# Counting edges between nodes in a four-layer graph network: 128 edges and four destinations per item, four items to a PSUM bank

## The reference

```
edge_index = stack([src, dst])
# layer 0: norms = segment_sum(exp(scores), rows)[rows]; res = segment_sum(w * v, rows)
# layer 1: e = exp(edge_weights - segment_max(edge_weights, tgt)[tgt])
#          gamma = e / segment_sum(e, tgt)[tgt]
# layer 2: h_e = segment_sum(h[src], dst)
# layer 3: prop(h) = segment_sum(wn[:, None] * h[row], col), with deg = segment_sum(1, row)
```

## Time and profile before

| | |
|---|---|
| runs (us) | 1515.14, 1507.11, 1510.53; median 1510.53 |
| profiled execution | 1497.43 us, of which the span is 1495.7 us |
| mean granted TensorE clock | 0.93 |
| busy share of the span | PE 75%, PEld 44%, DVE 74%, ACT 49%, POOL 32% |
| chain that ended last, by engine | PE 41%, DVE 29%, ACT 18%, issue 7% |

### The profile page before, as it was taken

One profiled execution on the slowest core, in us unless ns is written; L12 is line 12 of the kernel. 1 busy time (PEld: TensorE's weight loads), 2 busy tenths in 40 slices (PEclk: granted clock), 3 DMA queues, 4 the chain that ended last, 5 costly groups with the idle time before them and its releaser, 6 DMA issues.

```text
span 1495.7 us, 25017 instructions
## 1 busy us (share of the span) xinstructions
PE 1121.4 (75%) x8719; PEld 662.8 (44%) x8719; DVE 1107.2 (74%) x1935; ACT 736.6 (49%) x1363; POOL 476.0 (32%) x217
## 2 busy tenths in 40 slices
PE   0772465777777897787878778788469799999993
PEld 0441243555444452122222122222259697778783
DVE  8883799899897446898998998888695554432376
ACT  1562343666665126988998899898210000001121
POOL 5101000011000006698999999898100000000000
PEclk9997687999999798999999999999689899999997
DMA  0001000000000242111111111111111100010111
GB/s 7 15 1 46 5 1 18 2 8 9 2 2 15 75 105 62 32 46 39 41 46 39 43 50 46 55 42 54 39 47 46 44 28 8 1 27 8 48 36 33
DMA packets 60616, 47.50 MB, mean 32 GB/s; under 512 B 30607, under 2 KB 58895, under 8 KB 60367
## 3 DMA queue, kind: packets, MB, share of 16 engines
q1 hardware_dynamic: 59022, 44.04, 10.3%
q0 software_dynamic: 1472, 1.85, 0.5%
HBM read 32.07 MB, written 13.79 MB: 31 GB/s over the span
## 4 chain that ended last, share of the span: by engine, by line
PE 41%; DVE 29%; ACT 18%; issue 7%; SPq 2%; DMA 1%; POOL 1%; ACTq 1%; DVEq 0%
PE PS L1208 16%; DVE Eb L1015 11%; ACT CT L455 6%; ACT Eb L980 6%; ACT Eb L982 5%; PE PS L426 4%; PE PS L429 4%; DVE mov L358 3%; PE PS L1564 3%; PE PS L929 2%; PE PS L749 2%; PE PS L918 2%; DVE oneS L358 2%; ACT Eb L984 1%; POOL Eb L856 1%
## 5 line engine op out<-in xcount | busy, mean ns | idle before, releaser
L856 POOL TENSOR_SCALAR Eb<-Eb 128x1024 f32<-128x1024 f32 (+4 forms) x164 | 403.8, 2477 | 51.4 <-ACT Eb L984 51.0
L1015 DVE SCALAR_TENSOR_TENSOR Eb<-Eb,PS 128x1024 f32<-128x1024 f32 (+4 forms) x350 | 365.1, 1083 | 45.4 <-ACT Eb L982 35.2
L455 ACT ACTIVATE CT<-PS 128x200 f32 x783 | 236.6, 338 | 224.6 <-PE PS L429 222.6
L426 PE MATMUL PS<-mov,oneS 128*128 128x200 f16 x1566 | 245.2, 258 | 124.4 <-DVE mov L358 83.6
L1208 PE MATMUL PS<-hs,CT 128*128 128x192 f16 (+3 forms) x2500 | 269.8, 271 | 5.9 <-DVE B L1409 2.7
L984 ACT ACTIVATE Eb<-PS,small 128x1024 f32<-128x1024 f32 (+5 forms) x257 | 246.7, 995 | 22.7 <-PE PS L929 18.7
L1208 PEld LDWEIGHTS PS<-hs,CT 128*128 128x128 f16 (+1 forms) x2500 | 233.0, 101 | 39.4 <-DVE B L1409 3.2
L429 PE MATMUL PS<-CT,identb 128*128 x783 | 203.4, 260 | 29.1 <-ACT CT L455 28.2
L929 PE MATMUL PS<-Qb,Kb 96*128 96x512 f16 (+3 forms) x700 | 197.8, 365 | 13.1 <-ACT Eb L984 9.1
L426 PEld LDWEIGHTS PS<-mov,oneS 128*128 128x128 f16 x1566 | 138.4, 101 | 154.4 <-DVE mov L358 141.1
L358 DVE TENSOR_TENSOR mov<-iotaM,keyT 128x1600 f16<-128x1600 int16 x197 | 193.6, 983 | 0.0
(11 more groups left out here) (253 smaller groups left out, 937.5 us busy)
## 6 DMA issues: line engine op xcount, KB each, us to landing
Kb<-kd SPq DMA_DIRECT2D x168, 96.0 KB, 1.9
qd<-QH SPq DMA_DIRECT2D x24, 96.0 KB, 1.9
kd<-QH SPq DMA_DIRECT2D x24, 96.0 KB, 2.1
XG<-x_d SPq DMA_DIRECT2D x12, 192.0 KB, 2.4
x_d<-XG SPq DMA_DIRECT2D x12, 192.0 KB, 1.8
hs<-t_d SPq DMA_DIRECT2D x12, 192.0 KB, 2.5
Qb<-qd SPq DMA_DIRECT2D x4, 384.0 KB, 3.5
CT<-x_d SPq DMA_DIRECT2D x1, 1200.0 KB, 8.6
```

The lines of the kernel that those rows point to most:

```text
L426: t.matmul(ps, K.oneS[:, g % 2, 2 * k + s, :], K.mov[:, g % 2, 2 * k + s, :], start=(s == 0), stop=False)
L455: a.activation(K.CT[:, :, bass.ds(vals[p - 4 * g], W)], K.bank(p % 4)[:, 0:25 * W].rearrange("p (a w) -> p a w", w=W), ACT.Copy).then_inc( ...
L856: g.tensor_scalar(e, e, ELO, None, ALU.max).then_inc(S("floored"), 1)
L1015: v.scalar_tensor_tensor(out=e, in0=e, scalar=EHI, in1=cn, op0=ALU.min, op1=ALU.mult).then_inc(S("weighed"), 1)
```

## The change

Except for the length of a row of CT and the place of `ndis`, it stays within the count stage.

- A chunk has 128 edges and a window four destinations: 782 chunks, 784 windows, 1565 items, NJ = 13 slots, the second run from item LH = 792.
- Eight items (four of each run, now in blocks of four and not interleaved one by one) are a set; 198 sets. DVE makes one `oneS` (8 x 128) and one `mov` (8 x 100) per set, into three buffers (`DEEP`) instead of two.
- A half of a set is four items of one run, whose windows lie within 16 destinations. They share a bank: 25 x 16 columns. Each item has one count matmul, which writes its four columns of each 16 at an offset from a register (none for the first); then one CT matmul of 400 columns and one eviction of 400 columns. There are 392 halves. `load_windows` is called for each half: four registers on TensorE, one on ACT.
- The window numbers are relative within a half: `turnW` subtracts the first item's from the other three in the matmul that turns them. All are turned at the start, into `wI0` and `wI`.
- The chunk index of an item is found by seven comparisons of 1664 slots with chunk ends (`past`) and 7 + 42 matmuls that sum them over the partitions.
- The item arithmetic moves: DVE keeps the high and low parts (`high`), POOL computes the key, TensorE turns two tiles of 128 x 128, ACT copies them out of PSUM.
- The gathers have two buffers. CT is zeroed as POOL 7000, DVE 16000, ACT 16350 float32 elements per partition instead of 18500, 16000 and 4700. A row of CT has 12 columns more (NPC = 3148). `ndis` is a part of `small`.
- Softmax steps stand at sets 18, 26, ... 114, item turns at sets 6, 22, ...

```diff
-CH = 256
-NC = 392
+NPC = NP + 12
+CH = 128
+NC = 782
-W = 8
-WS = 3
-LH = 393
+W = 4
+WS = 2
+LH = 792
-NJ = 7
+NJ = 13
...
+SETS = 198
+DEEP = 3
+TURN_AT = {16 * (j - 1) + 6: j for j in range(1, NJ)}
+SOFT_AT = {18 + 8 * k: k for k in range(13)}
...
 def build_gpsimd(g, K):
...
+    g.memset(K.CTf[:, 0:ZG], 0.0).then_inc(S("zero_g"), 1)
...
+    g.wait_ge(S("slot_w"), 1)
+    gather(0)
     for j in range(NJ):
+        if j + 1 < NJ:
+            g.wait_ge(S("slot_w"), 2)
+            if j:
+                g.wait_ge(S("key"), j)
+                g.wait_ge(S("lo"), j)
+            gather(j + 1)
+        gd = K.GD[:, j % 2, :]
+        g.wait_ge(S("gd_in%d" % (j % 2)), 16 * (j // 2 + 1))
+        g.tensor_scalar(K.dl[:, :], gd, K.win[:, j:j + 1], 1.0, ALU.subtract, ALU.add).then_inc(own.sem, own.up())
+        g.wait_ge(own.sem, own.n)
+        g.tensor_scalar(K.over[:, :], K.dl[:, :], 1.0, None, ALU.is_ge).then_inc(own.sem, own.up())
+        g.tensor_scalar(K.under[:, :], K.dl[:, :], float(W), None, ALU.is_le).then_inc(own.sem, own.up())
+        g.wait_ge(S("hi"), j + 1)
+        g.tensor_scalar(K.key[:, :], K.hi[:, j % 2, :], 1.0, None, ALU.mult).then_inc(own.sem, own.up())
+        g.wait_ge(own.sem, own.n)
+        g.tensor_tensor(K.key[:, :], K.dl[:, :], K.key[:, :], ALU.add).then_inc(own.sem, own.up())
+        g.tensor_tensor(K.over[:, :], K.over[:, :], K.under[:, :], ALU.mult).then_inc(own.sem, own.up())
+        g.wait_ge(own.sem, own.n)
         if j:
...
+            g.wait_ge(S("key_turned"), j)
+        g.tensor_tensor(K.va[:, :], K.over[:, :], K.key[:, :], ALU.mult).then_inc(S("key"), 1)
...
 def build_vector(v, K):
...
+    for t in range(7):
+        v.tensor_scalar(K.past[:, t, :], K.iotaS[:, :], K.le[:, t:t + 1], None, ALU.is_gt).then_inc(S("past"), 1)
...
+    v.wait_ge(S("passed"), 1)
+    slots(slice(0, 1), K.bank(5)[:, 0:1])
+    v.wait_ge(S("passed"), 2)
+    slots(slice(1, NJ), K.bank(4)[:, 0:NJ - 1])
+    v.memset(K.CTf[:, ZG:ZV], 0.0).then_inc(S("zero_v"), 1)
+    v.wait_ge(S("windows"), 1)
+    v.tensor_copy(K.wI0[:, :], K.bank(5)[0:1, 128:256]).then_inc(S("reg_set"), 1)
...
+    for s in range(SETS):
+        j, o = s // 16, 8 * (s % 16)
+        v.wait_ge(S("items"), j + 1)
+        if s >= DEEP:
+            v.wait_ge(S("counted"), before(2 * (s - DEEP) + 2))
+        one_hots(K.oneS[:, s % DEEP, :, :], K.iotaX[:, :], K.KL[:, j, 1, o:o + 8, :], 128)
+        one_hots(K.mov[:, s % DEEP, :, :], K.iotaM[:, :], K.KL[:, j, 0, o:o + 8, :], 25 * W).then_inc(S("one_hot"), 1)
+        if s % 16 == 1 and j + 1 < NJ:
+            high(j + 1)
+        if s in SOFT_AT:
+            soft_step(SOFT_AT[s])
...
 def build_tensor(t, K):
...
+    for i, g in enumerate(PRESENT):
+        if i + 1 < len(PRESENT):
+            nxt = load_windows(K, t, mybir.EngineType.PE, PRESENT[i + 1], 4)
+        s, r = g // 2, g % 2
+        ps = bank(g % 4)[:, 0:25 * 4 * W].rearrange("p (a c) -> p a c", a=25)
+        t.wait_ge(S("one_hot"), s + 1)
+        if g >= 4:
+            t.wait_ge(S("placed"), INDEX[g - 4] + 1)
+        for k in range(items_of(g)):
+            to = ps[:, :, 0:W] if k == 0 else ps[:, :, bass.ds(vals[k], W)]
+            t.matmul(to, K.oneS[:, s % DEEP, 4 * r + k, :], K.mov[:, s % DEEP, 4 * r + k, :].rearrange("p (a w) -> p a w", a=25),
+                     start=(k == 0), stop=False, skip_group_check=True)
+        if g >= 2:
+            t.wait_ge(S("placed"), INDEX[g - 2] + 1)
+        t.matmul(ps, K.identb[:, :], K.CT[:, :, bass.ds(vals[0], 4 * W)], start=False, stop=True, skip_group_check=True
+                 ).then_inc(S("counted"), 1)
...
 def build_scalar(a, K):
...
+    def keep_items(j):
+        a.wait_ge(S("key_turned"), j + 1)
+        a.activation(K.KL[:, j, :, :, :].rearrange("p k i two -> p (k i) two"), bcast_in(K.bank(6)[:, 0:256], 256, 2), ACT.Copy
+                     ).then_inc(S("items"), 1)
...
+    for i, g in enumerate(PRESENT):
+        if i + 1 < len(PRESENT):
+            nxt = load_windows(K, a, mybir.EngineType.Activation, PRESENT[i + 1], 1)
+        s = g // 2
+        a.wait_ge(S("counted"), i + 1)
+        a.activation(K.CT[:, :, bass.ds(vals[0], 4 * W)],
+                     K.bank(g % 4)[:, 0:25 * 4 * W].rearrange("p (a c) -> p a c", a=25), ACT.Copy).then_inc(S("placed"), 1)
```

More of the change, by code:

```diff
@@ L91, in fl, with items_of, before @@
     return ap.rearrange("p t d -> p (t d)")
[L96 to L102, removed]
+SETS = 198
+SLOTS = NJ * 128
+PRESENT = [g for g in range(2 * SETS) if 4 * (g // 2) + LH * (g % 2) < NI]
+INDEX = {g: i for i, g in enumerate(PRESENT)}
+DEEP = 3
+TURN_AT = {16 * (j - 1) + 6: j for j in range(1, NJ)}
+SOFT_AT = {18 + 8 * k: k for k in range(13)}
+def items_of(g):
+    first = 4 * (g // 2) + LH * (g % 2)
+    return min(4, NI - first)
+def before(g):
+    return sum(1 for p in PRESENT if p < g)
 def alloc_build(K, st):
@@ L108, in alloc_build @@
     K.iotaX = sb(st, "iotaX", [128, 128], I16)
[L110 to L116, removed]
+    K.KL = sb(st, "KL", [128, NJ, 2, 128, 2], I16)
+    K.GS = sb(st, "GS", [128, 2, CH], I32)
+    K.GD = sb(st, "GD", [128, 2, CH], I32)
@@ L125, in alloc_build @@
[L125 to L135 removed]
+    K.lo = sb(st, "lo", [128, 2, CH], F32)
@@ L136, in alloc_build @@
+    K.le = sb(st, "le", [128, 7], F32)
+    K.cc = sb(st, "cc", [128, 7], I32)
+    with ExitStack() as st2:
+        K.iotaS = sb(st2, "iotaS", [128, SLOTS], I16)
+        K.past = sb(st2, "past", [128, 7, SLOTS], F16)
+    K.oneS = sb(st, "oneS", [128, DEEP, 8, 128], F16)
+    K.mov = sb(st, "mov", [128, DEEP, 8, 25 * W], F16)
     K.wv = sb(st, "wv", [128, J], F32)
@@ L203, in build_vector @@
     step = own.sem
[L204 to L208, removed]
+    v.memset(K.lw[:, 6:7], 32000).then_inc(S("lw_set"), 1)
+    v.memset(K.zf[:, :], 0.0).then_inc(S("zf"), 1)
+    v.memset(K.oneh[:, :], 1.0).then_inc(step, own.up())
+    v.wait_ge(S("iota"), 2)
@@ L211, in build_vector @@
     v.wait_ge(step, own.n)
[L212 to L215, removed]
+    v.scalar_tensor_tensor(out=K.pF[:, 1:2], in0=K.pI[:, 2:3], scalar=4.0 * LH, in1=K.pF[:, 0:1], op0=ALU.mult, op1=ALU.add
+                           ).then_inc(step, own.up())
@@ L230, in build_vector @@
[L230 to L262, removed]
-                              bcast_in(K.bank(6)[:, 256 + 128 * sub:384 + 128 * sub], 128, 2))
-            v.tensor_copy(K.wI[:, 128 * j:128 * j + 128], K.bank(4)[0:1, 0:128]).then_inc(S("items"), 1)
@@ new lines, in build_vector, with slots @@
+    first = K.identf[:, 0:128:4].unsqueeze(2).to_broadcast([128, 32, 3])
+    v.wait_ge(step, own.n)
+    v.tensor_tensor(K.turnW[:, :].rearrange("p (m k) -> p m k", k=4)[:, :, 1:4],
+                    K.identf[:, :].rearrange("p (m k) -> p m k", k=4)[:, :, 1:4], first, ALU.subtract).then_inc(step, own.up())
+    def slots(cols, ps):
+        v.scalar_tensor_tensor(out=K.win[:, cols], in0=ps, scalar=-4.0, in1=K.i4[:, cols], op0=ALU.mult, op1=ALU.add
+                               ).then_inc(step, own.up())
+        v.wait_ge(step, own.n)
+        v.tensor_scalar(K.cI[:, cols], ps, float(NC - 1), None, ALU.min).then_inc(S("slot_w"), 1)
@@ L383, in build_tensor @@
 def build_tensor(t, K):
     S, bank = K.S, K.bank
-    t.wait_ge(S("ends"), 1)
-    t.matmul(bank(0)[:, 0:NC - 1], K.onesf[0:1, :], K.lwF[:, NC:2 * NC - 1], start=True, stop=True).then_inc(S("ends_all"), 1)
+    for t_ in range(7):
+        t.wait_ge(S("past"), t_ + 1)
+        m = t.matmul(bank(5)[:, 0:1], K.past[:, t_, 0:128], K.oneh[:, :], start=(t_ == 0), stop=(t_ == 6))
+    m.then_inc(S("passed"), 1)
+    for j in range(1, NJ):
+        for t_ in range(7):
+            m = t.matmul(bank(4)[:, j - 1:j], K.past[:, t_, 128 * j:128 * j + 128], K.oneh[:, :], start=(t_ == 0), stop=(t_ == 6))
@@ L388, in turn_items @@
+    m.then_inc(S("passed"), 1)
+    t.wait_ge(S("slot_w"), 1)
+    t.matmul(bank(5)[0:1, 128:256], K.win[:, 0:1], K.turnW[:, :], start=True, stop=True).then_inc(S("windows"), 1)
+    t.wait_ge(S("slot_w"), 2)
+    t.matmul(bank(4)[0:NJ - 1, 128:256], K.win[:, 1:NJ], K.turnW[:, :], start=True, stop=True).then_inc(S("windows"), 1)
     def turn_items(j):
```

208 lines of the change are left out of this document (100 added, 108 removed).

## The result

| | before | after |
|---|---|---|
| runs (us), first chip | median 1510.53 (1506.50 to 1515.14, 7 runs) | median 1520.64 (1518.22 to 1525.06, 7 runs) |
| profiled execution (span) | 1497.43 (1495.7) | 1519.76 (1518.0) |
| mean granted clock | 0.93 | 0.81 |

The ratio is 1.0072, 95% interval 1.005 to 1.0093: slower, where 1485 was forecast and faster had 0.68. The result lies inside the range, on the wrong side of no change. So the change costs between 4 and 14 us, and 36 us lie between forecast and median on the first chip.

What follows compares the result with a forecast made beforehand. Bound: TensorE's own order of issue with ACT's loop in it. Count stage 372 + 37 + 7 = 416 against 439.6 (-23), preparation -2.5, total -25.6: 1472 for the profiled execution, 1485 for the median; range 1435 to 1528.

Steps and rivals of the forecast that it cites:

- TensorE per half: Count stage, TensorE's queue: register load gap of 0.51 plus four address steps of 0.11 make 0.95 us; bounds 0.75 and 0.99.
- h: Count stage: TensorE's time for a half of a set, four items; forecast 0.95 us.
- The gap: Count stage: from a CT matmul to the next first count matmul, register load included; 0.51 us, unchanged.
- The four steps: Count stage: three count matmuls and the CT matmul with register addresses, 0.11 us each, between 0.06 and 0.12.
- 352h + 82: Count stage time in us as a function of a half's time; 0.95 gives 416.
- Rival A: Count stage: TensorE's queue runs ahead and hides the address steps; half 0.75 us, -91.5 us, 1419 us; chance 0.20.
- Rival B: Count stage: TensorE's clock stays at its lower level; half 1.09 us, +24 us, 1534 us; chance 0.20.
- Rival C: Count stage: address steps at upper bound, or clock partly lower; half 1.00 to 1.045, about 1510 us; chance 0.12.
- Stalls: Count stage: softmax steps interrupting DVE, with three buffers as cover, cost TensorE 24.4, 2.6, 2.6 and 7.7, sum 37 us.
- ACT and DVE: Count stage: eviction of 400 columns 0.50 us, DVE set 1.08 us, ACT loop 1.07 per two halves; neither sets the pace.
- Preparation: Before the count stage: less zeroing on POOL, first one-hot at 38 us instead of 40.4; -2.5, bounds -6 and +4.
- The sum: Whole kernel: count stage -23 us and preparation -2.5, total -25.6 us, median 1485.

Runs made afterwards that it cites:

- the repeated run: The kernel after, unchanged, run again on another chip beside the kernel before: 1502.67 us against 1496.28, ratio 1.0040 (1.0024 to 1.0056).

## Why the prediction was wrong

**The step that failed** is "TensorE per half": h = 0.95. It was 1.02 (1.035 as a mean). The gap was right (0.51 forecast, 0.52 measured). The four steps were put at 0.11, on the ground that the released step's 0.12 contained some way that a queue at work would not walk again; they took 0.125, above the upper bound. 0.07 us by 392 halves is 27 us: the whole of the forecast gain of 23 and 4 more. With h = 1.02 the prediction's own formula, 352h + 82, gives 441 us; the stage took 442.1. The rest of the mechanism stood as written; the term was mis-sized, and runs with fewer registers show what it is made of.

What this taught beyond the size is where the expected gain went. Per set the array has a third fewer columns, DVE 0.4 us less, and ACT two evictions for four. But the kernel before issued 4 address registers and one load per 1024 edge slots, this one 8 and two. In the kernel before, the four registers showed no price. From 262 to 480 us its CT matmul began 0.086 us behind the count matmul ahead of it (median), exactly as the second count matmul behind the first, which has no register. An item's three matmuls of 200 columns took 0.26 us together (302.12 to 302.38), longer than the 0.13 of one register. In the kernel after, a register has one matmul of 100 columns beside it, 0.045 us, and shows in full: eight at 0.13 and two loads at 0.33 are 1.70 of the set's 2.04 us. That the array's work hid the registers before is a reading of these steps; no run changed them in the kernel before.

**Rival A** (steps hidden, h = 0.75; its sum leaves out the -2.5 that it names and should give -94 and 1416) was wrong: the weight loads in pairs that spoke for it are of matmuls without a register between.

**Rival B** had its condition right and its price wrong. The clock did fall, to 0.54 over the stage, by the lower level of 1.2 GHz. The rival lets each step lengthen to the 0.15 of a weight load; but a step of 0.125 set by the queue already holds such a load, which took 0.10 in the rows above. With the clock at 1.00 the half was the same. The Trainium skill ("TensorE: Matmul & The Clock Gate", section "What's actually happening") says that the default is throttled and activity releases it; the windows at the end of this document agree (384 matmuls in 50 us at 1.00, 243 at 0.53), and no time follows from it here.

**Rival C** is what came: steps at their upper bound, h within 1.00 to 1.045, "about 1510", with a chance of 0.12 given to it. In h it was met, in time only where the kernel was run again (6.4 us from no change); on the first chip it was 10.1 and lay outside its 7.5. The measured 1.02 lay outside the bounds of 0.75 and 0.99: a single released instruction of the kernel before was too little to close the range with, and its 0.12 was nearer to the truth than the 0.11 taken.

**Stalls.** Forecast 24.4, 2.6, 2.6 and 7.7, in all 37 us; measured 21.8, 1.9, 2.6 and 7.3, in all 33.6. The formula, at h = 1.02, gives 34.5. The wait of the first softmax step is 20.1 us, forecast about 22. Right; with two buffers the stage was 12.9 us longer.

**ACT and DVE.** 400 columns took 0.504 us (forecast 0.50), a set on DVE 1.09 us from oneS to oneS where nothing holds it (1.08). Neither was late.

**Preparation.** Forecast 38, measured 42.6 and, repeated, 41.1, against 40.4 before: the sign was wrong here too. Timeline of the kernel after:

```profile
1.19 5.67 POOL L177 IOTA iotaS<- 128x1664 int16 x1
...
7.52 9.90 DVE L279 TENSOR_SCALAR past<-iotaS,le 128x1664 f16<-128x1664 int16 x7
...
8.94 6.36 POOL L189 MEMSET CT<- 128x7000 f32 x1
...
17.53 2.56 PE L443 MATMUL PS<-oneh,past 128*128 128x1 f16 x81
...
25.08 13.39 DVE L298 MEMSET CT<- 128x16000 f32 x1 [3.28 <-issue]
...
42.62 0.69 DVE L394 TENSOR_TENSOR oneS<-iotaX,KL 128x1024 f16<-128x1024 int16 x1 [3.37 <-ACT KL L506]
```

POOL's memset took about what was forecast (6.4 for 5.9) but ended 5 us later (15.3 for 10), behind the new iota of 5.67 us, which my sum left out; three comparisons ran ahead of it at 0.56 each (forecast 0.6), the others waited until 15.30. The matmuls for the other slots were 84 and not 42, at under 0.04 (2.56 us for 81) instead of 0.1, so this came out about even; "7 + 42" in the list of the change should read 7 + 84. Last, DVE stood 3.28 us ahead of its memset with no cause in the trace, the same in the repeated run, and the cause stays open; its 13.4 us and the 4.2 behind it were as forecast. The comparisons ended 2.3 us later than forecast (17.3 for 15) and the memset began 5.1 later (25.1 for 20), which is the miss of 4.6 with the 0.5 that the rest was shorter.

**The sum.** Forecast -23 and -2.5. Measured in the repeated run +2.3 and +0.8: 3 us by the stages, 6.4 by the medians. About 2 of the other 3 may be the longer rows; that is not shown. The first chip's 10.1 us by medians stay partly open. No step of the prediction spoke of stalls in attention, and they are not simply the difference: the profile of the kernel after has 15 us of them and lies at its median, and that of the kernel before has none and lies 13 us below its own. Without the 15 us the kernel after would be at 1505, and the two would stand near the 1496 and 1503 of the other chips. So the timed runs of both may have had such stalls on the first chip. Only two profiles say so, and no run tested it.

## What to carry to other kernels

Count the register loads and the matmuls with an address in a register before counting columns: here each register cost 0.13 us of TensorE's queue, three times what the array needed for the matmul (0.045), and a load of four registers 0.33. Where the array had 0.26 us of matmuls per register, in the kernel before, the register did not show; so ask how much array work stands beside each. A change that halves the work of one matmul and doubles their number pays only while the queue is not the bound. Where "issue" ends a short wait that recurs with the period of a loop, move the queue's own instructions into a wait that is there anyway, or make fewer and larger register loads where no such wait is.

## What had not been expected

- The price of an address register is a rate and not a gap: half a set was 1.02, 0.90, 0.77, 0.635 us with four, three, two, one, though with two of them left the fourth count matmul began 0.043 behind the third, as if it had none.
- At half the clock (0.53) the count stage was as fast as at 0.96, 441.9 and 441.5 us.
- The clock rose where the queue got faster: with all offsets fixed, the same columns per set and 0.64 us per half, it was 1.00 in the stretch where the kernel after had 0.53.

That stretch in the windows view of the kernel with all offsets fixed, and of the kernel after:

```profile
300.00:350.00 50.00, 39.51 (x384) 20.76 (x385) 46.40 (x81) 39.24 (x80) 8.45 (x11) 1.00 0.01 2
```

```profile
300.00:350.00 50.00, 48.24 (x243) 25.33 (x242) 31.66 (x55) 24.55 (x49) 14.10 (x17) 0.53 0.05 15
```
